# Criss-cross attention: where the softmax weights are transposed, and where the column energies are masked and summed

## The chip, the cores and the metric

The kernel runs on one core of one Trainium2 chip. The metric is the device time of one execution in microseconds. Engines are called by their names in the profile: PE (TensorE matmul), PEld (its weight loads), DVE (VectorE), ACT (ScalarE), POOL (GpSimd) and SP (SyncE, which issues every DMA here).

## The reference, cut to what matters

```python
def _L0_conv_ref(x, Wq, bq, Wk, bk, Wv, bv, gamma):      # x: (8, 512, 96, 96) f32
    B, C, H, W = (8, 512, 96, 96)
    CQ = C // 8
...
    q = jnp.einsum('oc,bchw->bohw', Wq, x) + bq[None, :, None, None]
    k = jnp.einsum('oc,bchw->bohw', Wk, x) + bk[None, :, None, None]
    v = jnp.einsum('oc,bchw->bohw', Wv, x) + bv[None, :, None, None]
    energy_H = jnp.einsum('bchw,bcgw->bhwg', q, k)
    energy_H = energy_H - NEG * eye[None, :, None, :]
    energy_W = jnp.einsum('bchw,bchv->bhwv', q, k)
    att = jax.nn.softmax(jnp.concatenate([energy_H, energy_W], axis=-1), axis=-1)
    att_H, att_W = (att[..., :H], att[..., H:])
    out_H = jnp.einsum('bcgw,bhwg->bchw', v, att_H)
    out_W = jnp.einsum('bchv,bhwv->bchw', v, att_W)
    return gamma * (out_H + out_W) + x
```

Each pixel of a 96x96 image attends to the 96 pixels of its column (`energy_H`, its own pixel masked out) and the 96 of its row (`energy_W`), with one softmax over the 192. Eight images (batches) of 512 channels.

## The kernel before

N is 96, CP is 384 (four image lines of 96 pixels, called a chunk), CHUNKS is 24, CT is 4 (512 channels in four groups of 128). The weights are applied to x itself and the value projection Wv comes afterwards, once for the sum of both directions. One batch has two stages:

- **Column stage.** For each of 96 image columns, 4 channel groups are multiplied with that column's 96x96 weights (`attend_column`, L881; the trace counts each f32 matmul as two instructions, so a chunk of four columns is 32). x comes in pieces of two columns (`load_xtc`, 96 partitions of 4096 B, 393,216 B each) into a ring of CRING = 6 places: three in `XT_r` and three in `XT_c`. DVE moves the even columns out of PSUM, ACT the odd ones, four copies each (`move_column`, L679 and L505), into `Y`.
- **Row stage.** The same for 96 rows (`attend_row`, L900, pieces of two rows in a ring of RRING = 3 places, PSUM banks RBANKS = 3), DVE adds the result to `Y` (`add_row`, L687), ACT and DVE split `Y` in a high and a low part (`round_y` L516, `low_y` L616), and PE projects with Wv (`project`, L912, four output groups of 36 instructions counted with the low weight in each chunk). DVE adds bias and x (`finish`, L696).

Inside the row stage of batch b lie the q, k, energies and exponentials of batch b+1: in chunks n = 6 to 17 two chunks each of projection and row energies (`a_chunks`), in n = 18 to 22 five groups each of column energies (`b_groups`; four in n = 22). For batch 0 this work is a prologue ahead of everything.

Energies take this way: PE (`row_energies` L840, `column_energies` L849) to PSUM; `shift` on DVE takes the maximum over 96 keys (L625) and subtracts it into a slot of `E` (L630, four slots); `exponentials` on ACT (L486, one instruction of 96x384); for columns `mask` on POOL sets the diagonal to zero afterwards (L381); `sum_z` on DVE sums (L639); SP stores to `e_scratch` in DRAM, 96 partitions of 1536 B to a chunk. Once all sums of a batch are there, `factors` and `factors_of_columns` turn maxima and sums into two tables `F` (DVE, with a transpose L861 on PE for the row table).

Weights take this way in both stages: `load_p` reads a chunk of energies into `Pe` (three slots, 1536 B to a partition, 36,864 B apart in DRAM); `scale` on POOL multiplies with `F` (L390); `turn` on PE makes four 96x96 transposes (L867) into PSUM bank 7; `copy_turned` on ACT brings them to `Pt` (L499); then the chunk is attended. There are 48 chunks of weights in a batch (24 for columns, 24 for rows).

Every engine's order is written out by hand; an engine waits on semaphores at the head of each step, and what stands behind waits too. SP's queue is one such order: `load_p(b, i)` waits until chunk i-3 is turned, and loads of x are queued behind it. At the start of the row stage, rows 0 to 2 wait until every column has been moved, since they use the same PSUM banks.

## Time and profile before

| | us |
|---|---|
| median of 3 runs | 3886.9 (3885.88 to 3889.6) |
| the profiled execution, its own time | 3887.74 |
| its span | 3885.9 |
| PE busy | 3809.0 (98%) |
| DVE busy | 2430.1 (63%) |
| ACT busy | 1662.6 (43%) |
| POOL busy | 625.9 (16%) |

The share of busy time is an average over stages. The timeline gives for each instruction (or run of equal ones) its start and its length, and in brackets how long the engine had been idle and who ended that. The chain of work that ended last is followed back from the last instruction. The windows view gives the busy time of every engine in a stretch, with the TensorE clock granted (1.00 is full), the share of the DMA engines' time taken by packets, and their rate. That share goes over 1 where packets of one engine overlap.

### The profile page before, as it was taken

What the parts mean: (1) busy time and instruction counts of PE and PEld (TensorE: products, weight loads), DVE (VectorE), ACT (ScalarE), POOL (GpSimd) and SP (SyncE); (2) the same over time, 40 slices, a digit from 0 to 9 for tenths busy, and PEclk for the clock granted to TensorE, in tenths of its full rate; (3) what the DMA queues carried; (4) which work ended last, traced back from release to release, by engine and by line L of the source; (5) the groups of instructions that cost most, each with busy time, mean ns of one, the idle gap of its engine ahead of it and who ended that gap; (6) DMA issues with size and microseconds to landing.
All of it is one profiled execution on the core that took longest, in us unless ns stands there. A gap on an engine that the chain in (4) does not pass through costs nothing.

```text
span 3885.9 us, 72644 instructions
## 1 busy us (share of the span) xinstructions
PE 3809.0 (98%) x28440; PEld 3780.9 (97%) x28440; DVE 2430.1 (63%) x5084; ACT 1662.6 (43%) x3658; POOL 625.9 (16%) x793
## 2 busy tenths in 40 slices
PE   7799999999999999999999999999999999999999
PEld 7799999999999999999999999999999999999999
DVE  8646675466754677546684567845767456674554
ACT  8533454244542445424454244542444424444111
POOL 0410023100221003210032100320004200042000
PEclk9899999999999999999999999999999999999999
DMA  7687768777687775977759677597775977668665
GB/s 257 168 220 248 245 209 221 220 248 248 198 232 223 247 238 195 240 225 239 249 184 246 223 247 241 194 240 226 240 243 183 240 234 248 224 197 239 208 205 167
DMA packets 256803, 874.33 MB, mean 225 GB/s; under 512 B 34256, under 2 KB 108496, under 8 KB 256464
## 3 DMA queue, kind: packets, MB, share of 16 engines
q1 hardware_dynamic: 256464, 869.67, 72.4%
q8 instruction: 230, 3.77, 0.4%
q14 instruction: 109, 0.89, 0.1%
HBM read 661.92 MB, written 207.62 MB: 224 GB/s over the span
## 4 chain that ended last, share of the span: by engine, by line
PE 94%; DVE 5%; issue 1%; ACT 1%; DMA 0%; POOL 0%; SPq 0%; DVEq 0%; ACTq 0%; POOLq 0%
PE bank L912 41%; PE bank L881 18%; PE bank L900 17%; PE bank L830 9%; PE bank L867 3%; PE bank L849 3%; PE bank L840 3%; DVE Sx L611 1%; DVE E L630 1%; DVE mx L625 1%; DVE zs L639 1%; DVE Sx_first L611 0%; DVE Sy L616 0%; DVE Y L696 0%; DMA XT_c<-in_x_col 0%
## 5 line engine op out<-in xcount | busy, mean ns | idle before, releaser
L912 PE MATMUL bank<-Sy,Wv_hi 128*128 128x384 f32 x6144 | 1596.3, 340 | 11.9 <-DVE Sy L616 11.9
L912 PEld LDWEIGHTS bank<-Sy,Wv_hi 128*128 128x128 f32 x6144 | 1088.7, 189 | 13.1 <-issue 13.1
L912 PE MATMUL bank<-Sy,Wv_lo 128*128 128x384 f32 x3072 | 1029.7, 335 | 0.0
L696 DVE SCALAR_TENSOR_TENSOR Y<-bank,bv_sb,Y 128x384 f32<-128x384 f32 x768 | 471.9, 614 | 872.2 <-PE bank L912 871.6
L390 POOL TENSOR_TENSOR Pe<-Pe,F 96x384 f32<-96x384 f32 x384 | 320.1, 835 | 2634.9 <-DMA Pe<-e_scratch 2601.2
L900 PE MATMUL bank<-Pt,XT_r 128*128 128x96 f32 x6144 | 725.0, 275 | 7.8 <-ACT Y L505 5.4
L900 PEld LDWEIGHTS bank<-Pt,XT_r 128*128 128x128 f32 x6144 | 705.0, 192 | 10.8 <-issue 6.6
L516 ACT ACTIVATE Sy<-Y 128x768 fp32r<-128x768 f32 x384 | 302.8, 835 | 897.2 <-PE bank L912 862.2
L679 DVE COPY Y<-bank 128x96 f32<-128x96 f32 x1536 | 317.9, 321 | 442.7 <-PE bank L881 442.7
L912 PEld LDWEIGHTS bank<-Sy,Wv_lo 128*128 128x128 f32 x3072 | 577.2, 188 | 0.0
L505 ACT ACTIVATE Y<-bank 128x96 f32<-128x96 f32 x1536 | 322.2, 360 | 373.4 <-PE bank L881 373.4
L687 DVE TENSOR_TENSOR Y<-bank,Y 128x384 f32<-128x384 f32 x768 | 393.7, 548 | 31.7 <-PE bank L900 31.7
L616 DVE TENSOR_TENSOR Sy<-Y,Sy 128x768 fp32r<-128x768 f32 x384 | 367.2, 958 | 33.8 <-ACT Sy L516 33.8
L830 PE MATMUL bank<-Sx,Wqk_hi 128*128 128x384 f32 x1440 | 375.7, 342 | 12.3 <-DVE Sx L611 12.3
L486 ACT ACTIVATE E<-E 96x384 f32<-96x384 f32 x384 | 200.2, 521 | 401.4 <-DVE E L630 401.2
L881 PE MATMUL bank<-Pt,XT_r 128*128 128x96 f32 x3072 | 366.6, 276 | 0.0
L881 PE MATMUL bank<-Pt,XT_c 128*128 128x96 f32 x3072 | 364.3, 275 | 1.5 <-issue 1.3
L881 PEld LDWEIGHTS bank<-Pt,XT_r 128*128 128x128 f32 x3072 | 355.8, 193 | 0.0
L881 PEld LDWEIGHTS bank<-Pt,XT_c 128*128 128x128 f32 x3072 | 353.2, 192 | 2.1 <-issue 1.8
L611 DVE TENSOR_TENSOR Sx<-XA,Sx 128x768 fp32r<-128x768 f32 x348 | 321.1, 964 | 1.5 <-ACT Sx L471 1.5
L471 ACT ACTIVATE Sx<-XA 128x768 fp32r<-128x768 f32 x348 | 274.8, 837 | 6.2 <-DMA XA<-in_x 2.0
L479 ACT ACTIVATE KQ<-bank,bqk_sb 128x384 f32<-128x384 f32 x192 | 111.6, 581 | 370.8 <-PE bank L830 369.2
(62 smaller groups left out, 3219.2 us busy)
## 6 DMA issues: line engine op xcount, KB each, us to landing
XT_r<-in_x_row SPq DMA_DIRECT2D x384, 384.0 KB, 5.5
Y<-in_x SPq DMA_DIRECT2D x192, 768.0 KB, 6.1
out<-Y SPq DMA_DIRECT2D x192, 768.0 KB, 3.6
XA<-in_x SPq DMA_DIRECT2D x180, 768.0 KB, 7.0
XT_r<-in_x_col SPq DMA_DIRECT2D x192, 384.0 KB, 6.7
XT_c<-in_x_col SPq DMA_DIRECT2D x192, 384.0 KB, 6.2
e_scratch<-E SPq DMA_DIRECT2D x384, 144.0 KB, 2.6
Pe<-e_scratch SPq DMA_DIRECT2D x384, 144.0 KB, 7.4
```

The source lines that it names most:

```text
L390: nc.gpsimd.tensor_tensor(Pe[:, i % PRING, :, :], Pe[:, i % PRING, :, :], f, ALU.mult)\
L505: last = nc.scalar.activation(to[:, t, :, :], oc_ps[i % CBANKS][:, t * N:(t + 1) * N].rearrange("p (n r) -> p n r", r=ROWS), ACT.Copy)
L516: nc.scalar.activation(Sy[:, 0, cts, :], Y[:, n + 1, cts, :], ACT.Copy).then_inc(y_hi_made, 1)
L611: nc.vector.tensor_tensor(sx(a, m)[:, 1, cts, :], xa(a, m)[:, cts, :], sx(a, m)[:, 0, cts, :].bitcast(F32), ALU.subtract).then_inc(x_lo_ma ...
L616: nc.vector.tensor_tensor(Sy[:, 1, halves[h], :], Y[:, n + 1, halves[h], :], Sy[:, 0, halves[h], :].bitcast(F32), ALU.subtract).then_inc(y ...
L679: last = nc.vector.tensor_copy(to[:, t, :, :], oc_ps[i % CBANKS][:, t * N:(t + 1) * N].rearrange("p (n r) -> p n r", r=ROWS))
L687: nc.vector.tensor_tensor(at, or_ps[i % RBANKS][:, 0:CT * N].rearrange("p (t n) -> p t n", t=CT), at, ALU.add).then_inc(r_added, 1)
L696: nc.vector.scalar_tensor_tensor(at, proj_ps[c % 2][:, 0:CP], bv_sb[:, c:c + 1], at, op0=ALU.add, op1=ALU.add).then_inc(out_made, 1)
L830: last = nc.tensor.matmul(ps[:, 0:CP], w[:, ct, :], sx(a, m)[:, lo, ct, :], start=(ct == 0 and n == 0), stop=(ct == CT - 1 and n == 2))
L881: last = nc.tensor.matmul(oc_ps[i % CBANKS][:, ct * N:(ct + 1) * N], column_piece(j)[:, u, ct * P:(ct + 1) * P], Pt[:, g % 2, r * N:(r + 1 ...
L900: last = nc.tensor.matmul(or_ps[i % RBANKS][:, ct * N:(ct + 1) * N], XT_r[:, j % RRING, u, ct * P:(ct + 1) * P], Pt[:, n % 2, r * N:(r + 1 ...
L912: last = nc.tensor.matmul(proj_ps[c % 2][:, 0:CP], w[:, ct, at], Sy[:, lo, ct, :], start=(ct == 0 and k == 0), stop=(ct == CT - 1 and k == 2))
```

## The change

- **Blocks.** `E` and `Pe` are seen as three blocks of 32 keys: within a partition the order is now block, line, key, in place of line, key. The stores of energies put the three blocks of a partition at three places in DRAM (512 B each), laid out so that `load_p` reads one stretch of 147,456 B for a chunk, and 32x32 blocks transposed in place give the whole transpose. Partition p of block b then holds queries 3p, 3p+1 and 3p+2.
- **Turn.** `turn` is now one DVE instruction to a chunk (STREAM_TRANSPOSE, 96x384), written straight to `Pt` with a stride of three elements. PE's 192 transposes to a batch and ACT's 48 copies from PSUM are gone, with the bank that held them. In the column stage it stands ahead of DVE's two moves, in the row stage between `finish` 1 and 2.
- **Mask and sum of columns.** `mask` now writes -10000 ahead of the exponential. ACT takes the exponential of a column group in four instructions of 96x96, each with its sum (`accum_out`), and DVE's `sum_z` remains for rows only.
- **Factors.** The tables must have the permuted query order: `choose_factors` on ACT lays out a permuted identity, and PE makes each table with three matmuls; the row statistics are transposed a chunk earlier.
- **Moves and banks.** `move_column` is one instruction of 384 elements in place of four of 96. Rows have four banks, of which the first is the bank set free by the turn; row 0 waits only for `F`, rows 1 to 3 each for the column whose bank they take.

```diff
-    e_dram = nc.dram_tensor("e_scratch", (2, B, N, N, N), F32, kind="Internal").ap()
+    e_dram = nc.dram_tensor("e_scratch", (2, B, CHUNKS, BLOCKS, N, ROWS * BLOCK), F32, kind="Internal").ap()
...
-        oc_ps, or_ps, proj_ps = (*bank[0:3], bank[5]), bank[0:RBANKS], bank[3:5]
...
+        oc_ps, or_ps, proj_ps = (*bank[0:3], bank[5]), (bank[7], *bank[0:3]), bank[3:5]
...
             def store_column_energies(a, g):
-                sp.wait_ge(c_masked, past(c_masked, a * CHUNKS + g + 1))
-                sp.dma_start(e_dram[0, a, :, g * ROWS:(g + 1) * ROWS, :], E[0:N, g % ERING, :, :])\
+                sp.wait_ge(e_exped, past(e_exped, e_no(a, CHUNKS + g)))
+                sp.dma_start(e_dram[0, a, g, :, :, :].rearrange("b i x -> i b x"),
+                             E[0:N, g % ERING, :].rearrange("p (b x) -> p b x", b=BLOCKS))\
                     .then_inc(e_stored[g % ERING], 16)
 
             def load_p(b, i):
                 along, n = i // CHUNKS, i % CHUNKS
                 sp.wait_ge(p_turned, past(p_turned, p_no(b, i - PRING)))
                 e_landed(sp, b, n if along else CHUNKS + n)
-                sp.dma_start(Pe[:, i % PRING, :, :], e_dram[along, b, :, n * ROWS:(n + 1) * ROWS, :])\
+                sp.dma_start(Pe[:, i % PRING, :],
+                             e_dram[along, b, n, :, :, :].rearrange("b (p q) x -> (b p) (q x)", q=BLOCKS))\
                     .then_inc(p_in[i % PRING], 16)
...
             def mask(a, g):
-                pool.wait_ge(e_exped, past(e_exped, e_no(a, CHUNKS + g)))
-                at = E[0:N, g % ERING, :, :]
-                nc.gpsimd.affine_select(out=at, in_=at, compare_op=ALU.not_equal, fill=0.0, base=0,
-                                        pattern=[[0, ROWS], [-1, N]], channel_multiplier=1).then_inc(c_masked, 1)
+                pool.wait_ge(e_shifted, past(e_shifted, e_no(a, CHUNKS + g)))
+                at = by_block(E[0:N, g % ERING, :])
+                nc.gpsimd.affine_select(out=at, in_=at, compare_op=ALU.not_equal, fill=-1.0e4, base=0,
+                                        pattern=[[-BLOCK, BLOCKS], [0, ROWS], [-1, BLOCK]], channel_multiplier=1)\
+                    .then_inc(c_masked, 1)
...
             def exponentials(a, i):
-                act.wait_ge(e_shifted, past(e_shifted, e_no(a, i)))
-                at = E[0:N, i % ERING, :, :]
-                nc.scalar.activation(at, at, ACT.Exp).then_inc(e_exped, 1)
+                if i < CHUNKS:
+                    act.wait_ge(e_shifted, past(e_shifted, e_no(a, i)))
+                    at = E[0:N, i % ERING, :]
+                    nc.scalar.activation(at, at, ACT.Exp).then_inc(e_exped, 1)
+                else:
+                    g = i - CHUNKS
+                    act.wait_ge(c_masked, past(c_masked, a * CHUNKS + g + 1))
+                    at = by_row(E[0:N, i % ERING, :])
+                    for r in range(ROWS):
+                        last = nc.scalar.activation(at[:, r, :, :], at[:, r, :, :], ACT.Exp,
+                                                    accum_out=zs_c[0:N, g * ROWS + r:g * ROWS + r + 1])
+                    last.then_inc(e_exped, 1)
...
-            def copy_turned(b, i):
-                act.wait_ge(p_turned, past(p_turned, p_no(b, i)))
-                act.wait_ge(o_summed, past(o_summed, o_no(b, (i - 2) * ROWS + ROWS - 1)))
-                nc.scalar.activation(Pt[0:N, i % 2, :], t_ps[0:N, 0:CP], ACT.Copy).then_inc(pt_made, 1)
...
-                else:
-                    dve.wait_ge(c_masked, past(c_masked, a * CHUNKS + n + 1))
-                nc.vector.tensor_reduce(zs[:, along, n * ROWS:(n + 1) * ROWS], E[0:N, i % ERING, :, :], AX_X, ALU.add)\
...
+            def turn(b, i):
+                dve.wait_ge(p_scaled, past(p_scaled, p_no(b, i)))
+                dve.wait_ge(o_summed, past(o_summed, o_no(b, (i - 2) * ROWS + ROWS - 1)))
+                nc.vector.transpose(Pt[0:N, i % 2, :].rearrange("j (r p q) -> j q r p", r=ROWS, q=BLOCKS),
+                                    by_block(Pe[:, i % PRING, :])).then_inc(p_turned, 1)
 
             def move_column(b, i):
                 dve.wait_ge(o_summed, past(o_summed, o_no(b, i)))
                 to = Y[:, 1:, :, :].rearrange("p n t (r w) -> p t n r w", w=N)[:, :, :, :, i]
-                for t in range(CT):
-                    last = nc.vector.tensor_copy(
-                        to[:, t, :, :], oc_ps[i % CBANKS][:, t * N:(t + 1) * N].rearrange("p (n r) -> p n r", r=ROWS))
-                last.then_inc(c_moved_dve, 1)
+                nc.vector.tensor_copy(to, oc_ps[i % CBANKS][:, 0:CT * N].rearrange("p (t n r) -> p t n r", t=CT, r=ROWS))\
+                    .then_inc(c_moved_dve, 1)
...
+                turn(b, 0)
+                take_factors(b, 1)
                 for j in range(2):
                     out_landed(dve, b - 1, CHUNKS - 3 + j)
                 for i in range(ERING):
                     e_landed(dve, b, 2 * CHUNKS - ERING + i)
                 for g in range(CHUNKS):
+                    turn(b, g + 1)
...
+                    if turn_now:
+                        shift(b + 1, 2 * CHUNKS - 1)
+                        factors(b + 1)
                     finish(b, n, 0)
...
+                        factors_ready(b + 1)
                     finish(b, n, 1)
                     if b_now:
                         shift(b + 1, CHUNKS + b_now[1])
-                        sum_z(b + 1, CHUNKS + b_now[0])
-                    if turn_now:
-                        factors_of_columns(b + 1)
                     if a_now:
                         sum_z(b + 1, a_now[0])
+                    if n + 3 < CHUNKS:
+                        turn(b, CHUNKS + n + 3)
                     finish(b, n, 2)
...
-            def turn(b, i):
-                pe.wait_ge(p_scaled, past(p_scaled, p_no(b, i)))
-                pe.wait_ge(pt_made, past(pt_made, p_no(b, i - 1)))
-                for r in range(ROWS):
-                    last = nc.tensor.transpose(t_ps[0:N, r * N:(r + 1) * N], Pe[:, i % PRING, r, :], ident[:, :])
-                last.then_inc(p_turned, 1)
...
+            def turn_factors(a, along):
+                pe.wait_ge(f_ready, a * 2 + along + 1)
+                if not along:
+                    pe.wait_ge(f_chooser, a + 1)
+                for q in range(BLOCKS):
+                    last = nc.tensor.matmul(f_ps[along][:, q * N:(q + 1) * N], Kg[0:N, along, q * N:(q + 1) * N],
+                                            ident[:, :] if along else st[0:N, 1, :], start=True, stop=True)
+                last.then_inc(f_turned, 1)
...
-                if i < RBANKS:
-                    pe.wait_ge(c_moved_act, past(c_moved_act, (b + 1) * (N // 2)))
-                    pe.wait_ge(c_moved_dve, past(c_moved_dve, (b + 1) * (N // 2)))
+                if i == 0:
+                    pe.wait_ge(f_made, past(f_made, b * 2 + 2))
+                elif i < RBANKS:
+                    moved = c_moved_dve if i % 2 else c_moved_act
+                    pe.wait_ge(moved, past(moved, (b + 1) * (N // 2) - (RBANKS - 1 - i) // 2 - (1 - i % 2)))
                 else:
                     pe.wait_ge(r_added, past(r_added, b * N + i - RBANKS + 1))
```

Three places in the engines' orders show it. PE, batch 0, from the last column energies into the column stage (L867 transposes `Pe`; L881 attends columns), before:

```order
L849 MATMUL bank<-Kg,Q 96x96 x96
L856 MATMUL bank<-ident,mx 96x96
L857 MATMUL bank<-ident,zs 96x96
L861 MATMUL bank<-ident,st 96x96
L867 MATMUL bank<-ident,Pe 96x96 x8
L881 MATMUL bank<-Pt,XT_r 128x96 x16
L867 MATMUL bank<-ident,Pe 96x96 x4
L881 MATMUL bank<-Pt,XT_r 128x96 x8
```

and with the change, where L901 makes the factor tables and L916 attends:

```order
L886 MATMUL bank<-Kg,Q 96x96 x96
L893 MATMUL bank<-ident,mx_r 96x96
L894 MATMUL bank<-ident,zs_r 96x96
L901 MATMUL bank<-st,Kg 96x96 x3
L901 MATMUL bank<-ident,Kg 96x96 x3
L916 MATMUL bank<-Pt,XT_r 128x96 x24
L916 MATMUL bank<-Pt,XT_c 128x96 x24
```

The transposes between the chunks are gone, and the row of attending matmuls has nothing between its pieces.

DVE in the same place, before (L679 moves columns, L687 adds rows):

```order
L665 RECIPROCAL st<-st 96x96
L668 TENSOR_TENSOR F<-st 96x96
L669 TENSOR_TENSOR st<-st 96x96
L673 COPY F<-bank 96x96
L679 COPY Y<-bank 128x24x4 x192
L687 TENSOR_TENSOR Y<-bank,Y 128x4x96 x5
```

and with the change, where L712 is the turn and L718 the move:

```order
L696 RECIPROCAL st<-st 96x96
L698 TENSOR_TENSOR st<-st 96x96
L699 TENSOR_TENSOR Kg<-st 96x288
L706 COPY F<-bank 96x288
L712 STREAM_TRANSPOSE Pt<-Pe 96x3x128
L706 COPY F<-bank 96x288
L712 STREAM_TRANSPOSE Pt<-Pe 96x3x128
L718 COPY Y<-bank 128x4x24x4 x2
```

One turn now stands ahead of each pair of moves, and DVE waits in it for POOL's scaled weights.

ACT at the end of the column energies of batch 1 (chunk n = 21 before; n = 22 and 23 behind it), before (L493 gathers q, L486 is the exponential, L516 rounds `Y` for the next chunk's projection):

```order
L493 ACTIVATE Q<-KQ 64x384
L486 ACTIVATE E<-E 96x384
L493 ACTIVATE Q<-KQ 64x384
L486 ACTIVATE E<-E 96x384
L516 ACTIVATE Sy<-Y 128x768 x2
L499 ACTIVATE Pt<-bank 96x384
L493 ACTIVATE Q<-KQ 64x384
L486 ACTIVATE E<-E 96x384
```

and with the change, to the end of the batch's row stage (L533 gathers, L524 is a quarter of an exponential with its sum, L548 rounds):

```order
L533 ACTIVATE Q<-KQ 64x384
L524 ACTIVATE E,zs_c<-E 96x3x32 x4
L533 ACTIVATE Q<-KQ 64x384
L524 ACTIVATE E,zs_c<-E 96x3x32 x8
L548 ACTIVATE Sy<-Y 128x768 x2
L524 ACTIVATE E,zs_c<-E 96x3x32 x4
L552 ACTIVATE Kg<-ident 96x288
L557 ACTIVATE st<-st 96x192
```

The copy to `Pt` is gone from behind the rounding, and four short exponentials stand in the place of each long one, eight of them right ahead of the last rounding.

## Rows read from the trace of the kernel before

**Rows 1.** The page's head: span, and busy time (share of the span) of engines.

```profile
span 3885.9 us, 72644 instructions
...
PE 3809.0 (98%) x28440; PEld 3780.9 (97%) x28440; DVE 2430.1 (63%) x5084; ACT 1662.6 (43%) x3658; POOL 625.9 (16%) x793
```

**Rows 2.** The chain that ended last, share of the span by engine and by line.

```profile
PE 94%; DVE 5%; issue 1%; ACT 1%; DMA 0%; POOL 0%; SPq 0%; DVEq 0%; ACTq 0%; POOLq 0%
PE bank L912 41%; PE bank L881 18%; PE bank L900 17%; PE bank L830 9%; PE bank L867 3%; PE bank L849 3%; PE bank L840 3%; DVE Sx L611 1%; DVE E L630 1%; DVE mx L625 1%; DVE zs L639 1%; DVE Sx_first L611 0%; DVE Sy L616 0%; DVE Y L696 0%; DMA XT_c<-in_x_col 0%
```

**Rows 3.** The chain in order of time, batch 1's column stage: start, length, what.

```profile
634.02 0.33 PE bank L867 x4
634.35 3.57 PE bank L881 x32
637.93 0.33 PE bank L867 x4
```

**Rows 4.** Groups: line, engine, names, shapes, count | busy, mean ns | idle before.

```profile
L687 DVE TENSOR_TENSOR Y<-bank,Y 128x384 f32<-128x384 f32 x768 | 393.7, 548 | 31.7 <-PE bank L900 31.7
...
L616 DVE TENSOR_TENSOR Sy<-Y,Sy 128x768 fp32r<-128x768 f32 x384 | 367.2, 958 | 33.8 <-ACT Sy L516 33.8
...
L505 ACT ACTIVATE Y<-bank 128x96 f32<-128x96 f32 x1536 | 322.2, 360 | 373.4 <-PE bank L881 373.4
...
L679 DVE COPY Y<-bank 128x96 f32<-128x96 f32 x1536 | 317.9, 321 | 442.7 <-PE bank L881 442.7
...
L639 DVE TENSOR_REDUCE zs<-E 96x4 f32<-96x384 f32 x384 | 207.9, 541 | 12.4 <-POOL E L381 6.4
L486 ACT ACTIVATE E<-E 96x384 f32<-96x384 f32 x384 | 200.2, 521 | 401.4 <-DVE E L630 401.2
...
L867 PE MATMUL bank<-ident,Pe 96*96 96x96 f32 x1536 | 190.8, 246 | 5.7 <-ACT Pt L499 4.7 <-POOL Pe L390 1.0
...
L493 ACT ACTIVATE Q<-KQ 64x384 f32<-64x384 f32 x192 | 172.9, 904 | 83.5 <-PE bank L849 79.2
```

**Rows 5.** Landing times of the column pieces (L239), 20 us windows from 620 on.

```profile
DMA to landing us min/median/max: 5.5/8.7/9.6
...
DMA to landing us min/median/max: 7.0/7.5/8.3
...
DMA to landing us min/median/max: 5.8/6.4/6.8
...
DMA to landing us min/median/max: 4.6/5.1/5.8
```

**Rows 6.** The same for batch 0, window 203 to 223.

```profile
DMA to landing us min/median/max: 7.0/7.4/7.6
```

**Rows 7.** Windows of a column stage and of chunk n = 20: busy, clock, DMA.

```profile
640.00:660.00 20.00, 20.00 (x187) 20.00 (x186) 8.27 (x41) 10.37 (x48) 4.70 (x6) 1.00 1.04 259
...
561.60:577.40 15.80, 15.80 (x126) 15.72 (x126) 13.72 (x25) 9.17 (x14) 7.92 (x11) 1.00 0.61 197
```

(After the window and its length stand PE, PEld, DVE, ACT and POOL busy, then the clock, the DMA share and GB/s.)

**Rows 8.** Timeline of PE where one stage ends and the next begins.

```profile
610.94 0.59 PE L912 MATMUL bank<-Sy,Wv_hi 128*128 128x384 f32 x2 [1.40 <-DVE Sy L616]
...
618.34 0.29 PE L861 MATMUL bank<-ident,st 96*96 96x96 f32 x1 [0.71 <-DVE st L669]
...
620.59 0.49 PE L867 MATMUL bank<-ident,Pe 96*96 96x96 f32 x4
621.75 0.51 PE L867 MATMUL bank<-ident,Pe 96*96 96x96 f32 x4 [0.67 <-ACT Pt L499]
622.09 3.74 PE L881 MATMUL bank<-Pt,XT_r 128*128 128x96 f32 x32
...
717.17 3.78 PE L900 MATMUL bank<-Pt,XT_r 128*128 128x96 f32 x32 [0.80 <-ACT Y L505]
```

**Rows 9.** Timeline of DVE in the prologue's column energies, two groups in a row.

```profile
117.96 0.54 DVE L625 TENSOR_REDUCE mx<-bank 96x4 f32<-96x384 f32 x1
...
119.54 0.54 DVE L625 TENSOR_REDUCE mx<-bank 96x4 f32<-96x384 f32 x1
```

## Predicted before the kernel ran

> **What bounds the kernel now.** I read the head of the page first, then the chain that ended last, then the chain in order of time through a column stage, and last the waits at the places where one stage follows another. PE is busy for 3809.0 of 3885.9 us and the chain lies on it for 94% of the span [rows 1, 2]. So the other engines cost nothing until PE waits for them. In the column stage the chain is a strict alternation: 0.33 us of transposes (L867), 3.57 us of attending (L881), 0.33 us again [rows 3]. The period is 3.90 us. What leaves PE there shortens the span one for one, unless something else is late by then. In the stretches with energies DVE is well loaded (13.72 of 15.80 us in chunk n = 20) and ACT less (9.17) [rows 7].
>
> The second thing to see is DMA. In the column stage its share of time is 1.04 at 259 GB/s, while PE is never idle [rows 7]. A chunk there needs two pieces of 393,216 B and one load of weights of 147,456 B, 933,888 B in 3.905 us, which is 239 GB/s. The landing times tell the rest: in windows of 20 us their median falls from 8.7 to 7.5, 6.4 and 5.1 us [rows 5]. The stage starts with a backlog, and DMA works it off. The landing time falls by 1.2 us in 20, so DMA delivers 6% more than is asked for: its limit for this mix is an estimated 239/0.94 = 254 GB/s.
>
> **What leaves PE.** 48 turns to a batch at 0.33 us; from start to start over a whole period it is 3.905 - 3.57 = 0.334. The group has 1536 transposes, 4 x 48 x 8 [rows 4]. The first two turns of a batch stand in a gap that stays: before, the first turn starts at 620.59, the second waits 0.67 us for ACT's copy, and attending starts at 622.09, 1.5 us later [rows 8]. After, DVE does the last `finish` and then the turn; both handle 384 elements, 1.2 us together and some waits for semaphores, so the gap is about as long. That leaves 46 x 0.334 x 8 = **-122.7 us**.
>
> **What the turn costs on DVE.** No row has a DVE transpose. The nearest are 384 elements to a partition at 0.54 to 0.55 us (L687, L639) and 768 elements at 0.96 (L616) [rows 4]. I take 0.6, with 0.54 and 0.96 as ends; nothing lets it come below the pass over 384 elements. The moves fall from four pieces to one: four are 4 x 317.9/1536 = 0.83 us on DVE (L679) and 0.84 on ACT (L505); one piece of 384 should lie between 0.55 and 0.85. DVE's column load is then 0.6 + 2 x 0.7 = 2.0 us of 3.57, at the upper ends 2.7. It is covered, and so is the order: chunk g+1's turn begins when chunk g-1's last column is done, at the start of chunk g, and PE wants it 3.57 us later; column 4g is moved behind it by some 2 us, and its bank is wanted at 3.57. SP's next load of weights waits for the turn, with loads of x behind it, but these wait for columns of chunk g ended 1.79 us into it, so even 0.96 us holds nothing up. In the row stage DVE gains 0.6 us a chunk and in chunk n = 20 loses five sums of 0.54. **0 us.**
>
> The Trainium skill, page "VectorE: DVE Perf Modes", section "Rules for kernel authors", speaks against this change: it would have a 128x128 transpose done by TensorE where PSUM will do, and keeps DVE's for single 32x32 blocks. Here the row in question is the 0.33 us that PE pays on the path, against a DVE that is busy 63% of the span. By that rule the change would give nothing, by the rows the 122.7 us above; the rule weighs one transpose and not which engine is the bound.
>
> **What is next late: DMA in the column stage.** Without turns PE asks for 933,888 B in 3.57 us, 261 GB/s, more than 254. The chunk then takes 3.905 x 0.94 = 3.67 us, 0.10 more than PE needs: 2.4 us in 24 chunks. And the start is tighter. A piece's place is free five pieces before it is wanted: 5 x 1.95 = 9.76 us before, 5 x 1.785 = 8.93 after, while the slowest landings are 9.6 [rows 5]. That is 0.7 us more. Some batches' backlogs fell somewhat faster, so I take 3.0 us for each of seven batches. Batch 0 begins with little backlog but its landings stand at 7.0 to 7.6 us late in the stage and no longer fall [rows 6], so its limit is about 239 GB/s, and its slack is used up part of the way through: 3 us too. **+24 us**, with 0 as one end (the weights' loads may be faster in their new layout) and 35 as the other. In the row stage a chunk asks for less (197 GB/s in chunk n = 20, share 0.61 [rows 7]), and its 0.33 us are gained whole.
>
> **Where stages meet.** Row 0 now has the free bank, and the wait of 0.80 us for ACT's last move [rows 8] goes: 8 x 0.8 = **-6.4 us**. The wait of 0.71 us for the row factors [rows 8] should go, since the statistics are turned a chunk earlier; but six matmuls take the place of one transpose, three of them on the path ahead of the last projection at up to 3.57/16 = 0.22 us each [rows 3], less the 0.08 of the transpose: 7 x (0.71 - 0.58), **-1 us**. The wait of 1.40 us ahead of the last projection [rows 8] grows: ACT rounds `Y` there, and now stands behind the mask and four short exponentials instead of one. Roughly 0.85 us, seven times, **+6 us**. In the chunks before it the attending of two rows covers the same delay.
>
> **ACT's quarters and the prologue.** No row has a sum inside an exponential. The nearest rows for a short ACT instruction are L505, 96 elements every 322.2/1536 = 0.21 us, and L486, 0.521 us for 384 elements [rows 4]. A quarter lies between 0.21 and 0.52; I take 0.24, near the row with its size. In the prologue DVE turns out a group every 1.58 us, by 0.55 + 0.55 + 0.54 overlapped [rows 9]. The sum leaves DVE, and ACT becomes the bound with its gather of 0.90 and four quarters: 0.90 + 0.96 = 1.86 us. 24 x 0.28 = **+7 us**, with 3 and 34 as ends (0.21 and 0.52). In chunk n = 20 ACT goes from 9.17 us to 9.17 + 5 x 0.44 = 11.4 of 15.4: covered. Stores of 512 B pieces cost DMA more packets, in stretches whose share is 0.61; no price taken, 0 to 5 us in the prologue.
>
> **Sum.** -122.7 + 24 - 6.4 - 1 + 6 + 7 = -93. From the profiled execution's 3887.7 that gives 3794.6, and the median of the runs is 0.8 us lower than that execution: **3794 us**.
>
> **Rivals.**
> - *The column stage stays on PE.* The weights' loads are 15.8% of a chunk's bytes. They read 147,456 B in one stretch now, not rows 36,864 B apart. If that takes 0.10 us off their 0.58 us share of a chunk, DMA keeps up. For it: 0.10 is little. Against it: the bulk, the x pieces, is as before. It would give 3794 - 24 = 3770, with the prologue's lower end 3766. The Trainium skill, "DMA: Bandwidth & Descriptors", "Latency and other measured facts", says that widely pitched rows lower the rate and advises contiguous tiles, which is in favour of this rival; its pitches are other ones than here.
> - *Dearer quarters or a tighter DMA.* Quarters of 0.35 to 0.45 us: prologue +20 to +30 instead of 7, the last projection another 0.5 to 0.8 us seven times; or DMA at its 35. 3810 to 3840.
> - *Slower than before: ACT becomes the bound of the column energies.* In chunks n = 18 to 21 of seven batches ACT has 1.6 (rounding) + 5 x (0.90 + 4q) us of work in a period of 15.4. From q = 0.46 on it is late. At q = 0.60 it is 18.1, 2.7 us late 28 times (76 us), the prologue loses 24 x 1.7 = 41, the last projection 7 x 1.3 = 9 more: 3794 - 7 + 126 = 3913. It decides from about q = 0.57. Against it: a quarter would have to cost more than the whole exponential does now.
> - *The turn does not leave the path.* If DVE took over 3.57 us for a turn and two moves, the columns would go at its pace. At the upper ends it is 2.7 us, so this needs a transpose of 1.9 us. At 2.2 us nothing would be gained in columns: the 64 us that the sum has for them less the 24 of DMA would be lost: 3794 + 40 = 3834, inside the range of the second rival.
>
> **How the numbers follow.** Forecast (DMA sets the columns' pace, 3783 to 3808): 0.5. Columns on PE (3760 to 3783): 0.2. Dearer quarters, tighter DMA or a slow turn (3808 to 3850): 0.22. The gain gone within 0.2% (7.8 us, about what a measurement of this kernel can tell from no change): 0.03. Slower: 0.05. The range is 3765 to 3830; it leaves out the two last cases and the ends of the second and third, some 0.17. Faster 0.92, same 0.03, slower 0.05.
>
> **What the changed profile would show.** No transposes on PE but those of the statistics. In the chain in order of time, attending in column stages either in one piece (PE's bound) or with waits for DMA of x pieces, and a chunk's period of 3.67 us. Landing times there that stay at 8 to 9 us in place of falling to 5: that shows DMA's limit, and falling times refute it. A turn of 0.55 to 0.96 us, one move of 0.55 to 0.85. A quarter exponential every 0.21 to 0.3 us and a prologue group every 1.8 to 2.0 us. Row 0 without a wait for ACT. The prediction is wrong at its root if PE's waits in the column stage name DVE or POOL, or if attending matmuls themselves take longer than 3.57 us for 32.

## The result, and the profile after

The changed kernel takes **3779.6 us** (median of 4 runs, 3775.2 to 3781.0) against 3886.8 (4 runs, 3885.9 to 3889.6). The ratio is 0.9721, with a 95% interval from 0.9704 to 0.9738. The forecast was 3794 in a range of 3765 to 3830: direction and range held, and the gain is 107 us where the sum had 93. The profiled execution took 3778.9 us, with a span of 3777.1.

The head of the page after, and the chain that ended last by engine and by line (L949 projects, L916 attends columns, L937 attends rows, L867, L877 and L886 make keys, queries and energies):

```profile
span 3777.1 us, 68419 instructions
...
PE 3700.7 (98%) x26992; PEld 3681.1 (97%) x26992; DVE 2606.8 (69%) x4132; ACT 1644.5 (44%) x3474; POOL 637.8 (17%) x793
...
PE 94%; DVE 3%; ACT 2%; DMA 1%; issue 1%; POOL 0%; SPq 0%; DVEq 0%; POOLq 0%; ACTq 0%
PE bank L949 42%; PE bank L916 18%; PE bank L937 17%; PE bank L867 9%; PE bank L877 3%; PE bank L886 3%; ACT E L524 1%; DMA XT_r<-in_x_row 1%; DVE Sx L645 1%; DVE E L666 1%; DVE Sx_first L645 0%; ACT Q L533 0%; DVE mx_r L661 0%; DVE zs_r L672 0%; DVE Sy L650 0%
```

PE has lost 108.3 us of busy time against [rows 1], and the span 108.8. It is still the bound. DVE has taken 177 us more, and its share of the chain has fallen from 5% [rows 2] to 3%. The chain in order of time shows the column stage of batch 0 as one piece and that of batch 1 as one but for its first chunks, and the row stage's alternation (start, length, what):

```profile
153.07 88.77 PE bank L916 x768
...
261.50 8.35 PE bank L949 x48
269.85 3.54 PE bank L937 x32
273.39 8.35 PE bank L949 x48
```

```profile
626.75 78.82 PE bank L916 x704
```

704 matmuls in 78.82 us are 22 chunks of 3.583 us, where [rows 3] had 3.57 + 0.33. A plain row chunk takes 273.39 - 261.50 = 11.89 us; before it took 12.26 (the same rows of the chain there). The groups that the change made or altered (columns as in [rows 4]):

```profile
L539 ACT ACTIVATE Y<-bank 128x384 f32<-128x384 f32 x384 | 325.6, 848 | 436.9 <-PE bank L916 436.9
...
L718 DVE COPY Y<-bank 128x384 f32<-128x384 f32 x384 | 317.8, 828 | 216.5 <-PE bank L916 197.7
...
L712 DVE STREAM_TRANSPOSE Pt<-Pe 96x384 f32<-96x384 f32 x384 | 267.4, 696 | 29.0 <-POOL Pe L422 2.7
```

```profile
L524 ACT ACTIVATE E<-E 96x96 f32<-96x96 f32 x768 | 207.5, 271 | 147.5 <-POOL E L411 142.7
...
L524 ACT ACTIVATION_READ_ACCUMULATOR E<-E 96x1 f32 x768 | 143.3, 187 | 0.0
```

The turn costs 0.70 us on DVE. The moves cost as one instruction what four did: 317.8 and 325.6 us in all, against 317.9 and 322.2 [rows 4]. A quarter exponential is two instructions, one of them a read of the accumulator.

Where the 108.8 us of span went, stage by stage. The times are from the timelines of PE. "Columns" is from a batch's first column matmul to its first projection, so in the kernel before it holds 25 of the batch's 48 turns; "rows" is from there to the next batch's first column matmul, or to the end, with 21 turns of this batch. The other two stand in the gap ahead of the batch. The prediction's 122.7 us of turns are split here by these counts, 66.8 and 55.9.

| | before | after | change | the sum had |
|---|---|---|---|---|
| prologue, to 142.98 / 153.07 | 143.0 | 153.1 | +10.1 | +7 |
| columns, 8 batches | 822.8 | 758.7 | -64.1 | -66.8 - 6.4 + 24 = -49.2 |
| rows, 8 batches | 2920.2 | 2865.3 | -54.9 | -55.9 - 1 + 6 = -50.9 |

So the rows came out 4 us better than summed, the prologue 3 us dearer, and the surprise, 15 us, is in the column stages. The landing times of the column pieces (L269, batch 1, windows of 20 us from 618 on) and the window that answers to [rows 7]:

```profile
DMA to landing us min/median/max: 5.6/8.0/9.9
DMA to landing us min/median/max: 6.8/7.1/7.6
DMA to landing us min/median/max: 6.0/6.5/7.0
DMA to landing us min/median/max: 6.0/6.2/6.5
```

```profile
640.00:660.00 20.00, 20.00 (x182) 20.00 (x181) 13.39 (x17) 9.66 (x12) 4.56 (x6) 1.00 1.04 268
```

They still fall, at 268 GB/s, with the same share of 1.04 as at 259 GB/s before. The prediction had named this as what would refute its DMA limit. (The 259 GB/s that [rows 7] shows before was itself above the 254 of that limit.)

Where the stages meet, batch 1 (timeline of PE; in brackets its idle time before the row, and what ended it):

```profile
605.91 0.81 PE L949 MATMUL bank<-Sy,Wv_hi 128*128 128x384 f32 x2 [2.26 <-DVE Sy L650]
...
613.82 0.67 PE L901 MATMUL bank<-st,Kg 96*96 96x96 f32 x6
...
617.97 5.57 PE L916 MATMUL bank<-Pt,XT_r 128*128 128x96 f32 x48 [0.84 <-issue]
...
705.41 7.68 PE L937 MATMUL bank<-Pt,XT_r 128*128 128x96 f32 x64
```

Against [rows 8]: the wait ahead of the last projection has grown from 1.40 to 2.26 us, the one for the row factors is gone, and so is the one for ACT's last move ahead of row 0.

### The profile page after: what moved, and what is told of

Same layout as the page of the kernel before. It is cut to its first block, busy times and chain, and to the rows that moved or that the text cites. A ratio compares the mean times of both kernels' runs of the same rounds, so it can differ in the third digit from the quotient of the medians.

```text
span 3777.1 us, 68419 instructions
## 1 busy us (share of the span) xinstructions
PE 3700.7 (98%) x26992; PEld 3681.1 (97%) x26992; DVE 2606.8 (69%) x4132; ACT 1644.5 (44%) x3474; POOL 637.8 (17%) x793
## 4 chain that ended last, share of the span: by engine, by line
PE 94%; DVE 3%; ACT 2%; DMA 1%; issue 1%; POOL 0%; SPq 0%; DVEq 0%; POOLq 0%; ACTq 0%
PE bank L949 42%; PE bank L916 18%; PE bank L937 17%; PE bank L867 9%; PE bank L877 3%; PE bank L886 3%; ACT E L524 1%; DMA XT_r<-in_x_row 1%; DVE Sx L645 1%; DVE E L666 1%; DVE Sx_first L645 0%; ACT Q L533 0%; DVE mx_r L661 0%; DVE zs_r L672 0%; DVE Sy L650 0%
## 5 line engine op out<-in xcount | busy, mean ns | idle before, releaser
L949 PE MATMUL bank<-Sy,Wv_hi 128*128 128x384 f32 x6144 | 1600.9, 341 | 18.4 <-DVE Sy L650 17.9
L949 PEld LDWEIGHTS bank<-Sy,Wv_hi 128*128 128x128 f32 x6144 | 1093.5, 189 | 19.9 <-issue 19.1
L949 PE MATMUL bank<-Sy,Wv_lo 128*128 128x384 f32 x3072 | 1031.9, 336 | 0.0
L734 DVE SCALAR_TENSOR_TENSOR Y<-bank,bv_sb,Y 128x384 f32<-128x384 f32 x768 | 471.8, 615 | 757.3 <-PE bank L949 757.1
L937 PE MATMUL bank<-Pt,XT_r 128*128 128x96 f32 x6144 | 717.4, 274 | 2.4 <-DMA XT_r<-in_x_row 2.2
L937 PEld LDWEIGHTS bank<-Pt,XT_r 128*128 128x128 f32 x6144 | 713.7, 192 | 3.8 <-DMA XT_r<-in_x_row 3.7
L548 ACT ACTIVATE Sy<-Y 128x768 fp32r<-128x768 f32 x384 | 302.3, 834 | 877.1 <-PE bank L949 850.5
L949 PEld LDWEIGHTS bank<-Sy,Wv_lo 128*128 128x128 f32 x3072 | 579.6, 189 | 0.0
L539 ACT ACTIVATE Y<-bank 128x384 f32<-128x384 f32 x384 | 325.6, 848 | 436.9 <-PE bank L916 436.9
L718 DVE COPY Y<-bank 128x384 f32<-128x384 f32 x384 | 317.8, 828 | 216.5 <-PE bank L916 197.7
L650 DVE TENSOR_TENSOR Sy<-Y,Sy 128x768 fp32r<-128x768 f32 x384 | 374.4, 977 | 64.0 <-ACT Sy L548 64.0
L867 PE MATMUL bank<-Sx,Wqk_hi 128*128 128x384 f32 x1440 | 374.6, 341 | 12.4 <-DVE Sx L645 12.4
L916 PE MATMUL bank<-Pt,XT_r 128*128 128x96 f32 x3072 | 357.7, 277 | 8.4 <-issue 8.4
L916 PEld LDWEIGHTS bank<-Pt,XT_r 128*128 128x128 f32 x3072 | 351.3, 193 | 10.2 <-issue 10.1
L916 PE MATMUL bank<-Pt,XT_c 128*128 128x96 f32 x3072 | 355.3, 275 | 4.2 <-issue 4.2
L916 PEld LDWEIGHTS bank<-Pt,XT_c 128*128 128x128 f32 x3072 | 348.9, 192 | 5.2 <-issue 4.9
L712 DVE STREAM_TRANSPOSE Pt<-Pe 96x384 f32<-96x384 f32 x384 | 267.4, 696 | 29.0 <-POOL Pe L422 2.7
```

The lines of the kernel that those rows point to most:

```text
L539: nc.scalar.activation(to, oc_ps[i % CBANKS][:, 0:CT * N].rearrange("p (t n r) -> p t n r", t=CT, r=ROWS), ACT.Copy).then_inc(c_moved_act, 1)
L548: nc.scalar.activation(Sy[:, 0, cts, :], Y[:, n + 1, cts, :], ACT.Copy).then_inc(y_hi_made, 1)
L650: nc.vector.tensor_tensor(Sy[:, 1, halves[h], :], Y[:, n + 1, halves[h], :], Sy[:, 0, halves[h], :].bitcast(F32), ALU.subtract).then_inc(y ...
L718: nc.vector.tensor_copy(to, oc_ps[i % CBANKS][:, 0:CT * N].rearrange("p (t n r) -> p t n r", t=CT, r=ROWS))\
L734: nc.vector.scalar_tensor_tensor(at, proj_ps[c % 2][:, 0:CP], bv_sb[:, c:c + 1], at, op0=ALU.add, op1=ALU.add).then_inc(out_made, 1)
L867: last = nc.tensor.matmul(ps[:, 0:CP], w[:, ct, :], sx(a, m)[:, lo, ct, :], start=(ct == 0 and n == 0), stop=(ct == CT - 1 and n == 2))
```

## The experiments

Each kernel was run beside the kernel before on the same chip; times are medians of at least 4 runs. "The changed kernel" is at 3779.6.

### Was it the layout of the weights that saved the column stages?

Two runs asked this from both sides: the changed kernel with loads of rows 36,864 B apart, and the kernel before with loads in one stretch.

```
- e_dram (2, B, CHUNKS, BLOCKS, N, ROWS * BLOCK)
+ e_dram (2, B, N, CHUNKS, BLOCKS * ROWS * BLOCK)
+ three stores a group in place of one, one for each block
```

> The changed kernel, but a chunk of energies lies in DRAM as before the change: its 96 rows of 1536 B are 36,864 B apart (the store of a chunk becomes three DMAs of 96 pieces of 512 B). Theory A (the single stretch of the weights' loads is what raised DMA's limit from 254 to some 268 GB/s, and so kept the columns on PE): landing times of the column pieces stay at 8 to 9 us through the stage, a chunk of columns takes 3.65 to 3.70 us instead of 3.58, and the time is 3795 to 3805. Rival B (254 was never the limit; DMA delivers more when more is asked for): landings as in the changed kernel (8, 7, 6.5), a chunk 3.58, the time 3780 within 5 us.

Measured: 3778.1 us (3774.3 to 3783.3), ratio 0.9720. All column stages stay between 3.57 and 3.60 us a chunk after their first four. The landings of batch 1, same windows as above:

```profile
DMA to landing us min/median/max: 7.7/8.2/10.3
DMA to landing us min/median/max: 7.3/7.6/8.0
DMA to landing us min/median/max: 7.0/7.4/7.8
DMA to landing us min/median/max: 8.1/8.8/9.2
```

They are somewhat later and rise at the end. Batch 1's column interval is 96.0 us for 94.9, but the eight intervals together come to 759.2 us for 758.7: next to nothing.

```
- e_dram (2, B, N, N, N), loads of [:, n * ROWS:(n + 1) * ROWS, :]
+ e_dram (2, B, CHUNKS, N, ROWS * N), loads of [n, :, :]
```

> The kernel before, with one edit: a chunk of energies lies in DRAM in one stretch of 147,456 B. Nothing else moves, PE's turns stay. Theory A: landing times in the column stage start at 8 to 9 us and fall by some 2.2 us in 20 instead of 1.2, under 5 us after 40. Rival B: they fall as in the kernel before (8.7, 7.5, 6.4, 5.1). Both expect the time of the kernel before, 3887 within 4 us, since PE hides it.

Measured: 3888.1 us, ratio 0.9999 (0.9990 to 1.0008). The landings of batch 1 have medians of 8.9, 8.0, 7.2 and 7.5 us, no earlier than with the pitch [rows 5]. So the pitch of the weights' loads decides nothing here, on either side. The layout was not what let the columns keep PE's pace. The Trainium skill's advice for contiguous tiles ("DMA: Bandwidth & Descriptors", section "Latency and other measured facts"), which the prediction counted for that rival, made no difference that these two runs can show.

### The turns alone

The kernel before, in its old layout and with three banks for rows, without the transposes. ACT copies a quarter as much in their place, and that an identity: this kernel leaves the softmax weights out of its output.

```
- for r in range(ROWS):
-     last = nc.tensor.transpose(t_ps[0:N, r * N:(r + 1) * N], Pe[:, i % PRING, r, :], ident[:, :])
- last.then_inc(p_turned, 1)
+ pe.sem_inc(p_turned, 1)
```

> The kernel before with the old layout and no turns at all: PE only signals, ACT copies a 96x96 identity to Pt, the rest of Pt is zero, so the weights are left out of the output. PE's order is otherwise as before. This asks DMA for 261 GB/s in the column stage with the old layout. Theory A: landings stay at 8 to 9 us, a chunk of columns takes 3.67 us, time 3887 - 128 + 24 = 3783 or more. Rival B: landings fall, a chunk takes 3.57 to 3.59, time about 3887 - 128 = 3759 to 3765.

Measured: 3801.7 us (3797.1 to 3804.0), ratio 0.9778. Two things follow. First, six of eight column stages run at 3.573 to 3.576 us a chunk after their start, the others at 3.60 and 3.76. In the six, at 261 GB/s asked for and in the old layout, PE sets the pace, so 254 GB/s is no fixed limit. But in batch 1, at 3.76, DMA does set it, at 250 GB/s, where it moved 274 in batch 2 with the same share of 1.04 (windows as in [rows 7], batch 1 and batch 2):

```profile
640.00:660.00 20.00, 20.00 (x177) 19.72 (x175) 8.87 (x44) 9.62 (x49) 4.93 (x6) 1.00 1.04 250
...
1100.00:1120.00 20.00, 20.00 (x181) 20.00 (x181) 9.10 (x44) 10.04 (x54) 4.94 (x6) 1.00 1.04 274
```

The first four chunks take 16.3 to 19.5 us where PE needs 14.3, and in batch 1 the landings don't fall:

```profile
DMA to landing us min/median/max: 5.5/9.3/10.6
DMA to landing us min/median/max: 8.4/8.8/9.2
DMA to landing us min/median/max: 8.7/9.0/9.5
DMA to landing us min/median/max: 8.9/9.5/9.7
```

Second, the turns are worth 86.6 us here (3888.3 - 3801.7), not the 122.7 of 46 x 0.334 x 8. Most of what is missing is in the columns: their intervals fall by 37.2 us (822.8 to 785.6) where 25 x 0.334 x 8 = 66.8 were to be had, and the slow starts are the larger part of the difference. The rest is in the row stage: the long chunks with row energies go from 17.87 to 17.73 us only, 0.14 for a turn of 0.33, while in the changed kernel they take 17.48. For these the bank was the next suspect.

### The fourth bank for rows

```
- RBANKS = 4;  or_ps = (bank[7], *bank[0:3])
+ RBANKS = 3;  or_ps = bank[0:3]
+ row 0 waits for all moves of the column stage, as before
```

> The changed kernel with three PSUM banks for rows and the old waits at the row stage's start (every column moved before row 0), the bank set free by the turn left unused. The prediction's term: 0.8 us more ahead of row 0 in each batch, +6.4 us in all, 3786. Rival: the pieces of the first rows are late anyway (the first four rows lost 0.3 to 0.6 us to DMA in the changed kernel), so that part of it is hidden and the time rises by 3 us or less.

Measured: **3822.0 us** (3818.4 to 3824.4), ratio 0.9832. The bank is worth 42 us, where the prediction had 6.4 for it. Part is what it foresaw: in the timeline of PE where batch 1's rows start, row 0 waits again.

```profile
712.74 5.57 PE L937 MATMUL bank<-Pt,XT_r 128*128 128x96 f32 x48 [1.13 <-ACT Y L539]
```

The larger part it did not. Attending of one long chunk in batch 1, on PE and beside it on DVE, with three banks:

```profile
806.52 3.93 PE L937 MATMUL bank<-Pt,XT_r 128*128 128x96 f32 x32
```

```profile
807.33 0.60 DVE L734 SCALAR_TENSOR_TENSOR Y<-bank,bv_sb,Y 128x384 f32<-128x384 f32 x1
807.85 0.94 DVE L650 TENSOR_TENSOR Sy<-Y,Sy 128x768 fp32r<-128x768 f32 x1
808.72 0.55 DVE L725 TENSOR_TENSOR Y<-bank,Y 128x384 f32<-128x384 f32 x1
```

and the same chunk in the changed kernel, on PE:

```profile
798.26 3.71 PE L937 MATMUL bank<-Pt,XT_r 128*128 128x96 f32 x32
```

A row is 8 matmuls, 0.89 us. The fourth needs the first one's bank 24 matmuls after the start, at 806.52 + 24 x 0.1115 = 809.20. But DVE had a `finish` and a `low_y` (L734, L650) ahead of the first row's addition, which ended at 808.72 + 0.55 = 809.27, 2.75 us after attending began. PE stands for 0.22 us there. The timeline has no row for it in this chunk, but it is seen in the length, 3.93 against 3.71, and in the starts of the matmuls in the trace: after the first they are 0.11 us apart, but for two steps of 0.26 and 0.19 just behind the 24th. All 77 long chunks of this run have such steps there, and so have all 77 of the run without turns; in the changed kernel none has. Of the 0.22 us these rows account for 0.07 (809.27 - 809.20); what the rest is, they don't show. In the kernel before, attending of such a chunk starts at 848.75 and the first addition starts at 850.60 and takes 0.55: 2.40 us after the start, 0.28 early, because PE had first spent 0.33 us on the turn. There 10 of 77 long chunks wait at that place, and the list of waits has one row for it, 1.3 us in five waits of up to 0.3:

```profile
PE bank L900 <- DVE Y L687: 1.3, 5, 0.3
```

**The transposes had been covering a wait for a bank in the other 67; taking them away uncovers it, and the fourth bank takes it away.** Between the two spans (3821.3 and 3777.1) 9.7 us lie in the column intervals (1.2 us a batch, where rows start) and 34.5 in the row stages: 11 long chunks of 0.24, four later ones of about the same, one of 0.5, and some 0.05 in most of the plain ones, which take 11.94 us with three banks and 11.89 with four.

### The loads ahead of the column stage

```
+ at n = CHUNKS - 1: load_xtc(b + 1, i) for i in range(RRING, CRING), ahead of the last store
```

> The changed kernel, but the first three pieces for XT_c of the next batch are issued ahead of the store of the last output chunk, not behind it. Theory: the wait early in the column stage (0.5 to 1.6 us in the first four chunks) is for pieces queued behind that store's 786,432 B, and comes down by 0.5 to 1.4 us seven times: 3770 to 3776. Rival: DMA as a whole is behind there, so another transfer is late instead and the time is that of the changed kernel.

Measured: 3779.8 us, ratio 0.9723: no change. The first four chunks of batches 2 to 4 take 14.34 us where they took 14.5 to 15.1, but later chunks give it back: in batches 3 and 6 they take 3.66 and 3.75 us each, where they took 3.58 and 3.60. An earlier transfer does not make the queue deliver more.

### ACT's quarters

Both kernels here have one exponential for a group of four columns, and DVE makes the sums. In the first everywhere, in the second in the prologue alone.

```
- for r in range(ROWS):
-     last = nc.scalar.activation(at[:, r], at[:, r], ACT.Exp, accum_out=zs_c[...])
+ nc.scalar.activation(at, at, ACT.Exp).then_inc(e_exped, 1)
+ DVE, a group later: tensor_reduce(zs_c[...], by_row(E[...]), AX_XY, ALU.add)
```

> The changed kernel, but a column group has one exponential of 96x384 after the mask, and DVE sums it, as before the change (turn, layout, banks and factors stay changed). The theory that the quarters with their sums cost the prologue 10 us and the wait ahead of the last projection 0.9 us seven times: prologue group back from 2.07 to about 1.6 us, that wait back from 2.3 to 1.4 us, the time 3780 - 10 - 6 = 3764. The rival, that DVE with the turn on it has no room for the sums (chunk n = 20 would have 14.9 of 15.5 us on DVE): waits of PE for DVE appear in chunks 18 to 22 and the time is 3775 or more.

Measured: 3778.1 us, ratio 0.9720. The first column stage starts at 142.8 us again, which is 10 us won. But the row stages lose as much: chunks n = 21 and 22 take 15.85 and 14.81 us instead of 15.39 and 13.81. DVE has the sums to make there, and PE waits in these two chunks 0.5 us for its shift and 0.5 us for its addition of a row, which it does not in the changed kernel. So the quarters are right in the row stage and wrong in the prologue. The other half of the expectation failed: the wait ahead of the last projection stays at 2.12 us with the quarters gone, since ACT, ahead of the rounding, now stands for POOL's mask.

```profile
593.95 0.52 ACT L524 ACTIVATE E<-E 96x384 f32<-96x384 f32 x1 [1.57 <-POOL E L412]
...
596.35 0.58 PE L963 MATMUL bank<-Sy,Wv_hi 128*128 128x384 f32 x2 [2.12 <-DVE Sy L648]
```

What made that wait grow is thus not the quarters alone.

> The changed kernel, but in the prologue alone a column group has one exponential and DVE sums it; in the batches ACT keeps the quarters. Theory: the prologue is ACT's with quarters (2.07 us a group) and gives back its 10 us, while the batches don't lose what the kernel with DVE sums everywhere lost (1.5 us a batch): 3769. Rival: the 1.5 us a batch there were not from the sums, then the time is 3778 again.

Measured: **3767.8 us** (3763.3 to 3769.6), ratio 0.9692 (0.9678 to 0.9707), 11.8 less than the changed kernel. What the quarters did in the prologue stands in ACT's timeline of the changed kernel, where ACT is never idle:

```profile
120.48 0.85 ACT L533 ACTIVATE Q<-KQ 64x384 f32<-64x384 f32 x1
121.36 0.28 ACT L524 ACTIVATE E<-E 96x96 f32<-96x96 f32 x1
121.55 0.19 ACT L524 ACTIVATION_READ_ACCUMULATOR E<-E 96x1 f32 x1
121.64 0.27 ACT L524 ACTIVATE E<-E 96x96 f32<-96x96 f32 x1
...
122.34 0.19 ACT L524 ACTIVATION_READ_ACCUMULATOR E<-E 96x1 f32 x1
122.55 0.85 ACT L533 ACTIVATE Q<-KQ 64x384 f32<-64x384 f32 x1
```

A group takes 122.55 - 120.48 = 2.07 us, and before 1.58 [rows 9]. 24 x 0.49 is 11.8 us; in the profiled executions the first column matmul starts at 142.3 us instead of 153.1, 10.8 sooner.

### The wait ahead of the last projection

In chunk n = 22 ACT rounds the next chunk's values ahead of the third group's quarters, not behind them.

```
- for g in b_now[:3]:            (then round_y(b, n + 1), then b_now[3:])
+ late = 2 if n == B_LAST else 3
+ for g in b_now[:late]:         (then round_y(b, n + 1), then b_now[late:])
```

> The changed kernel, but in chunk 22 ACT rounds Y for the last projection ahead of the third group's exponentials, not behind them. Theory: the wait ahead of the last projection (2.26 us in the changed kernel, 1.40 before) is ACT standing behind mask and exponentials, and comes back to 1.4 us: -6 us, 3774. Rival: what stands behind (exponentials, their stores, the factors) is then late for the tables and the same time is lost at the next batch's start: 3779.

Measured: **3769.6 us** (3766.3 to 3770.9), ratio 0.9698 (0.9683 to 0.9712), 10.1 less. The wait is back at its old size:

```profile
605.68 0.59 PE L950 MATMUL bank<-Sy,Wv_hi 128*128 128x384 f32 x2 [1.40 <-DVE Sy L651]
```

0.86 us seven times are 6.0 us. The other 4 are seen in windows of 5.3 us in the changed kernel that begin 0.24 us ahead of the first matmul after the wait (columns as in [rows 7]: the third number from the end is PE's granted clock), at the ends of batches 0, 2 and 3:

```profile
605.67:610.97 5.30, 5.06 (x20) 5.09 (x21) 4.04 (x11) 1.91 (x10) 0.58 (x1) 0.68 1.06 336
...
1532.28:1537.58 5.30, 5.07 (x29) 5.10 (x30) 3.94 (x11) 1.91 (x10) 0.58 (x1) 1.00 1.07 335
1994.26:1999.56 5.30, 5.05 (x20) 5.08 (x21) 4.03 (x11) 1.91 (x10) 0.58 (x1) 0.68 1.06 334
```

After the wait of 2.26 us the clock goes to its lower level (1.2 GHz) for a while in five of the seven batches: the mean over the window is 0.68, and 1.00 in the two others. Five other runs have the wait of 2.26 us, and their clock falls behind it in three or four batches of seven: 23 of 42 cases in all. The first pair of matmuls after it takes 0.81 us, and 0.59 at the full clock. After waits of 1.40 us it is 1.00 in all seven batches, both in the kernel before and in this one, and in the four other runs with that wait (42 cases):

```profile
605.44:610.74 5.30, 5.06 (x29) 5.09 (x30) 3.95 (x11) 2.81 (x18) 0.58 (x1) 1.00 1.08 328
```

The row stages show the price: 368.6 us with the lower clock (five batches of the changed kernel), 367.7 without it (two), 366.85 here (all seven). 5 x 0.9 + 7 x 0.86 = 10.5, measured 10.1. The Trainium skill, page "TensorE: Matmul & The Clock Gate", section "What's actually happening", says that the gate looks at how busy PE has been, at times that are not aligned with the kernel. That the same wait costs the clock in five batches and not in two agrees with it, but does not prove it.

### The merged moves

```
- one copy of 128x384 a column
+ four copies of 128x96 a column, on VectorE and on ScalarE
```

> The changed kernel, but the move of a column group's outputs out of PSUM is written as four instructions of 128x96 again, on VectorE and on ScalarE, in place of one of 128x384. The changed kernel's 384 moves took 317.8 us on VectorE and 325.6 on ScalarE, against 317.9 and 322.2 in four pieces before. Theory A (a move costs what its scattered write costs, by the element, and splitting it costs nothing that matters): 3780 us, within 3772 to 3786, ratio 0.972; the moves' groups again near 318 and 322 us, the columns at 3.573 us a chunk. Theory B (one instruction saves latency on the path to the banks, so that the merging was part of why the columns keep 3.573 us): 3.6 to 3.7 us a chunk, +4 to +20, 3784 to 3800.

Measured: 3782.8 us (3781.3 to 3786.7), ratio 0.9734 (0.9719 to 0.9748), 3 us above the changed kernel, with intervals that overlap. Column stages stay at 3.573 to 3.616 us a chunk. A gain from the merging is not shown: 3 us are less than these intervals can tell apart.

### Both repairs together

> The changed kernel with both repairs that helped alone: in the prologue one exponential for a group with the sums on VectorE (that alone gave 3767.8), and in chunk 22 the rounding of the next chunk's values ahead of the third group's exponentials (that alone gave 3769.6). Theory A (the two losses lie in different stretches and add up: -11.8 and -10.1 against 3779.6): 3758 us, 3754 to 3762, ratio 0.9668; column stage of batch 0 from about 142.3, a row stage of 366.85 us. Theory B (one gives back what the other saves, by transfers that come no sooner): 3764 to 3770.

Measured: **3758.4 us** (3755.6 to 3763.0), ratio 0.9671 (0.9656 to 0.9685). The two gains add up (-21.2, where -21.9 was summed). This version beats both kernels. The head of its page:

```profile
span 3761.2 us, 68275 instructions
...
PE 3686.6 (98%) x26992; PEld 3666.9 (97%) x26992; DVE 2623.3 (70%) x4156; ACT 1629.0 (43%) x3306; POOL 639.8 (17%) x793
```

PE is busy for 14 us less than in the changed kernel with the same 26992 matmuls, since fewer of them run at the lower clock (mean granted clock 0.995 for 0.989).

> As the kernel with both repairs, and the pieces of x for the column stage are loaded ahead of the last store of the stage before. Alone that gave 3779.8 against 3779.6, since what the first four chunks gained (14.34 us in place of about 15) later chunks gave back. Theory A (the queue has only so much to give, nothing gained): 3758 us, the same as without it. Theory B (with the other two repaired the start stall decides): 3750 to 3754, -0.6 us in each of seven batches.

Measured: 3760.0 us (3756.1 to 3764.5), ratio 0.9673. Its stages start at 14.34 to 14.9 us for four chunks in seven batches, and the chunks behind them take up to 3.76 us in a batch's mean. That is batch 0, where DMA sets the pace with landing times of 9.4 us and 237 to 242 GB/s at a share of 1.04 (from 180 to 220 us). The start of the stage was again not worth repairing by order alone.

## Why the prediction was right, and where it was not

**What leaves PE: right, but it leaned on a term that was mis-sized.** PE is the bound and its time came off: 0.33 us a column chunk, 0.37 a plain row chunk, 0.37 to 0.39 a long one. In the long chunks that held only because the fourth bank came with it. With three banks they win 0.14 us instead. The term "where stages meet" had it at 6.4 us, the wait that the trace of before showed; the run with three banks measured 42. The wait that it also prevents showed in the kernel before in 10 of 77 long chunks only, since in the others the transpose hid it, and the prediction did not read that row. Removing the turns alone gave 87 us, less also by its slow column starts. (Two small slips in the sum do not matter: 46 x 0.334 x 8 is 122.9 and not 122.7, and quarters of 0.21 us would cost the prologue 3.8 us and not 3.)

**What the turn costs on DVE: right.** 0.70 us for 0.6 in a range of 0.54 to 0.96; one move 0.83 where 0.55 to 0.85 was given, at its upper end. DVE's load in a column chunk is 0.70 + 2 x 0.83 = 2.4 of 3.57 us, and covered. By the rule quoted from the Trainium skill, "VectorE: DVE Perf Modes", section "Rules for kernel authors", the change would have given nothing. The measurement, 107 us, decides against it here, where PE was the bound.

**DMA in the column stage: wrong, the step that failed.** +24 us were summed, some 9 are there. The undisturbed column interval was 102.17 us (batches 2 and 5 of before). Without its 25 turns and the wait at row 0 it would be 26 chunks' worth of attending, 26 x 3.573 + 0.1 = 93.0, so 9.15 less; the mean fell by 64.1 / 8 = 8.0. Some 1.1 us a batch are lost beyond what was lost before, at the first four chunks (14.5 to 16.0 us for 14.3, batch 0 17.1), at single later chunks of batches 2, 5 and 6 (up to 4.5 us) and at the row pieces. The failed step is "DMA delivers 6% more than is asked for: its limit for this mix is an estimated 239/0.94 = 254 GB/s". Falling landing times say that the backlog shrinks; they don't say what the queue could deliver if more were asked for. At 268 GB/s they fell too. Nor is there one limit for this mix: at a share of 1.04 the windows show from 232 GB/s (before, batch 0, 206 to 226 us) to 274. In single stages the DMA-bound pace of the prediction did come, 3.76 us a chunk in batch 1 of the run without turns; in the changed kernel no stage was so slow. The run without turns and the run with the old pitch exclude that the new layout is the reason, so the rival "the column stage stays on PE" gave the right pace for a wrong cause. Its 3770 came out 10 too low: some 9 us for DMA stayed, and the prologue cost 3 more, less 4 that the rows gave.

**Where stages meet: the waits right, their consequence missed.** The wait ahead of the last projection was put at +0.85 us and is +0.86. Of its cause, mask and quarters, the runs show that without the quarters it stays at 2.12 us, and that rounding one group sooner brings it back to 1.40. That it would cost the clock was not foreseen, 0.9 us more in five batches. The factors' wait is gone as predicted.

**Quarters and the prologue: the mechanism right, the size off.** ACT became the bound there, as said. The quarter was taken at 0.24 us; it is 0.27 from start to start, and the last accumulator read adds some 0.1 before the next gather: 2.07 us a group for the 1.86 predicted. +10.1 us measured where the sum had 7.

**The errors, added up:** -14.9 in the columns, which is the DMA term (9 for 24), +3.1 in the prologue, -4.0 in the rows. In the rows several things cancel: chunks gain 0.37 to 0.39 us in place of 0.33, some 0.04 of it from the fourth bank. Chunk n = 22 loses 1.0 us in seven batches and chunk n = 23 loses 0.9 in five (12.79 to 13.81 and 11.17 to 12.08), some 12 us for the 5 of the sum. And the few long chunks that waited for a bank before, up to 18.35 us for 17.85, some 3.4 us in all, do so no more.

**Open.** Why batches 5 and 6 of the run without turns took 19.4 us for their first four chunks and the others 16.5 was not settled. In that run chunk n = 23 takes 9.67 us for 11.17, so its column stages begin 1.5 us sooner; how much of the slow starts that explains was not measured. What makes DMA deliver 250 GB/s in one stage and 274 in the next, and landing times of stages with the same layout differ by 2 us and more, is open too. The change of the factors' order and of the mask was run only together with the rest. Nor was it tried what the column stages would do with fewer bytes to load.

## What to carry to other kernels

Where work is taken off the bound engine, ask what that work was giving time to: the waits that it covers hardly show in the trace of before (here 1.3 us in the list, 34.5 once uncovered), so add up when the next buffer comes free against when it will now be wanted (here 809.27 against 809.20). A queue's capacity can't be read from landing times that fall; here it showed only where they stayed or rose while PE waited, and then differed from stage to stage. And look at edits that move a cost between engines stage by stage: the sums inside the exponential were right in the row stage and cost 12 us in the prologue, and the best kernel takes each where it fits.

## What the runs showed of the hardware

- A sum inside an exponential costs ScalarE a second instruction, 187 ns for the accumulator read beside 271 for 96x96; four of them in a row start every 0.27 us.
- A transpose of 32x32 blocks over 96x384 fp32 on VectorE took 0.70 us, against 0.55 for a pass over 384 elements with arithmetic.
- A move of 384 elements from a bank took 0.83 us on VectorE and 0.85 on ScalarE, and as much when written as four instructions of 96.
- A wait of 2.26 us on PE was followed by a stretch at 1.2 GHz (mean granted clock 0.68 over 5.3 us) in five cases of seven in the changed kernel and in 23 of 42 over six runs, a wait of 1.40 us in none of 42.
- At a DMA share of 1.04, windows of 20 us in column stages moved from 232 to 274 GB/s: neither that share nor one window's rate is a capacity.
- In the prologue, where PE is idle by turns, the mean clock fell from 0.88 to 0.50 once its groups came every 2.07 us in place of 1.58; PE was not the bound there:

```profile
110.00:153.00 43.00, 28.63 (x146) 24.21 (x145) 23.24 (x47) 35.51 (x164) 24.22 (x36) 0.50 0.33 86
```
